# Banded attention with a new schedule: values transposed, q and k halves swapped by DMA, clearing in parts

## The reference

```python
q = _apply_rope(proj(Wq, bq))      # 16 heads of 64 features
k = _apply_rope(proj(Wk, bk))      # rot = concat([-x2, x1]); x*cos + rot*sin
v = proj(Wv, bv)
# block of 128 queries against the block before and its own (256 keys), band mask
scores = einsum('bhnqd,bhnkd->bhnqk', qb, kcat) * scale
attn = softmax(where(valid, scores, -1e30))
ctx = einsum('bhnqk,bhnkd->bhnqd', attn, vcat)
return merged @ Wo.T + bo
```

## Time and profile before

| | us |
|---|---|
| median of 3 runs | 1757.1 (1752.41 to 1758.5) |
| the profiled execution | 1754.96 |
| its span, first to last instruction | 1753.2 |
| window stage, within the span | about 57 to 890 |

### The profile page before, as it was taken

How to read it: one execution, slowest core, us unless ns; L and a number is a source line. 1 busy time by engine, 2 the same in 40 slices (tenths; PEclk the granted TensorE clock), 3 DMA queues, 4 the chain that set the end, 5 groups by cost and what they waited for, 6 DMA issues and landing times. The chain is left out here.

```text
span 1753.2 us, 34607 instructions
## 1 busy us (share of the span) xinstructions
PE 1382.8 (79%) x9686; PEld 1165.0 (66%) x9686; DVE 1069.7 (61%) x3844; ACT 860.1 (49%) x1810; POOL 729.3 (42%) x725
## 2 busy tenths in 40 slices
PE   0799999999999999999944189962997974269791
PEld 0478787887878788787843188861584863258791
DVE  5566666666666666666667355538685877434553
ACT  1355555555555565656544044431684764134450
POOL 4355454545454555454537534540000005724451
PEclk9899999999999999999965599985998985579896
DMA  4899980000000000000031112213000001112125
GB/s 161 145 207 201 203 171 0 0 0 0 0 0 0 0 0 0 0 0 0 0 107 53 49 54 63 60 31 95 1 1 1 0 1 40 52 52 61 53 60 145
DMA packets 129148, 90.63 MB, mean 52 GB/s; under 512 B 9196, under 2 KB 121983, under 8 KB 128818
## 3 DMA queue, kind: packets, MB, share of 16 engines
q1 hardware_dynamic: 118560, 70.73, 18.9%
q0 software_dynamic: 9216, 16.94, 2.9%
q10 hardware_dynamic: 1298, 2.13, 0.4%
HBM read 30.28 MB, written 61.57 MB: 52 GB/s over the span
## 5 line engine op out<-in xcount | busy, mean ns | idle before, releaser
L598 ACT ACTIVATE sc<-sc,mx 128x256 f32<-128x256 f32 x516 | 234.4, 501 | 329.6 <-DVE mx L666 329.6
L765 POOL TENSOR_TENSOR rot<-rot,sin 128x512 f32<-128x512 f32 x132 | 209.5, 1587 | 365.3 <-DVE rot L675 365.3
L666 DVE CUSTOM_DVE_ANT_0 sc<-ps,mask 128x256 f32<-128x256 f32 x516 | 197.7, 420 | 185.8 <-PE ps L506 183.2
L529 PEld LDWEIGHTS po<-V,pT 128*128 128x128 f32 x2048 | 255.4, 193 | 5.3
L529 PE MATMUL po<-V,pT 128*128 128x65 f32 x2048 | 258.6, 269 | 0.0
L887 POOL DMA_INDIRECT yt<-yo,xt x160 | 160.2, 1001 | 205.3 <-DVE yo L987 175.8
L423 POOL DMA_INDIRECT xg<-xw,slot x128 | 124.9, 976 | 289.6 <-DVE slot L285 254.3
L506 PE MATMUL ps<-K,Q 64*128 64x256 f32 x1032 | 196.6, 431 | 0.8 <-DVE mx L666 0.7
L516 PE MATMUL pt<-ident,sc 128*128 128x128 f32 x1028 | 169.5, 288 | 13.9 <-ACT sc L598 13.9
L516 PEld LDWEIGHTS pt<-ident,sc 128*128 128x128 f32 x1028 | 108.1, 141 | 103.7 <-issue 59.3
L947 ACT ACTIVATE hT<-ph,b 128x256 f32<-128x256 f32 x320 | 125.8, 477 | 87.9 <-PE ph L910 87.9
(11 more groups left out here) (181 smaller groups left out, 2708.5 us busy)
## 6 DMA issues: line engine op xcount, KB each, us to landing
xg<-zeros SPq DMA_DIRECT2D x76, 520.0 KB, 9.7
xt<-xg SPq DMA_DIRECT2D x80, 130.0 KB, 2.1
got<-yt SPq DMA_DIRECT2D x32, 256.0 KB, 5.2
yt<-yo,xt POOLq DMA_INDIRECT x160, 2.3
x<-in_hidden SPq DMA_DIRECT2D x8, 256.0 KB, 8.4
w<-in_w SPq DMA_DIRECT2D x1, 2048.0 KB, 9.4
xg<-xw,slot POOLq DMA_INDIRECT x128, 2.3
out_x<-x SPq DMA_DIRECT2D x8, 256.0 KB, 4.3
```

Of the source, the lines that this page charges most:

```text
L529: ins = nc.tensor.matmul(po[:, b // 2, (b % 2 * 2 + h) * VCOLS:(b % 2 * 2 + h + 1) * VCOLS], pT[:, b % 2, h, kb, :], V[:, c, b + kb, h, :] ...
L598: nc.scalar.activation(sc[:, b % 2, h, :], sc[:, b % 2, h, :], ACT.Exp, scale=-1.0, bias=mx[:, b % 2, h:h + 1]).then_inc(S["p"], 1)
L666: nc.vector.tensor_tensor_reduce(sc[:, b % 2, h, :], ps[:, h, 0:2 * P], (mask0 if b == 0 else mask)[:, :], -float(HD) ** -0.5, 3e38, ALU.a ...
L765: nc.gpsimd.tensor_tensor(rot[:, which, :], rot[:, which, :], s.sin[:, pos(sb)], ALU.mult).then_inc(S["pool"], 1)
```

## The change

**Values and normalising.** V becomes the stationary operand (64 columns of a head) and the transposed probabilities the moving one (128 columns); the outputs of the two heads lie on partitions 0 to 63 and 64 to 127 of `po`, already transposed. V loses its column of ones; the sums come from the exponentials' accumulator (`ls`). DVE inverts them (`invert`, 128x8), POOL copies each over 64 columns (`spread`, 128x512 into `rb`), PE transposes that (`turn_sums`, block 3, into `pj`), ACT copies it to `rT` (`read_sums`), and DVE multiplies `po` by it once a unit (`normalise`, block 0 of the next unit), into `oT`. `project_out` moves to block 3 of the next unit. The bias of v is added in `keep_v`, that of the output by POOL (`add_bias`, 128x512, once in 8 units), and `start_out` goes.

**Order.** `scores` and `maxima` run three blocks ahead, with four buffers of `sc` instead of two; `project_q`, `project_k`, `project_v` stand in blocks 0, 1, 2.

**Rotation.** The host's permutation goes. The halves of 32 partitions are swapped by four DMAs of 32 partitions x 2 KB on SP's queue, for q and for k of each unit (`swap_halves`), from `lin` to `rot`. `lin` times cos goes to a tile of its own, `lc`. POOL's `rotate` is as before; `spread` stands between that of q and that of k.

**Clearing.** One DMA in each unit (`clear`, 5 or 4 blocks of 130 KB), behind the unit's swaps on SP's queue; 64 in all, the same bytes. SP also loads v's bias (512 KB) and the output's (64 KB), broadcast over the partitions, ahead of the stage.

```diff
             def project_q(v, c, sb, head=False):
-                pe.wait_ge(S["v_sb"], START + v + CHUNKS)
-                if not head:
-                    pe.wait_ge(S["oT_sb"], START + v - 1)
+                if head:
+                    pe.wait_ge(S["v_sb"], START + v + CHUNKS)
+                else:
+                    pe.wait_ge(S["r_sb"], START + v - 2)
...
+                    pe.wait_ge(S["norm"], START + u)
+                for kb in range(2):
+                    for h in range(2):
+                        ins = nc.tensor.matmul(po[h * HD:(h + 1) * HD, c % 2, b * P:(b + 1) * P], V[:, c, b + kb, h, :],
+                                               pT[:, b % 2, h, kb, :], start=(kb == 0), stop=(kb == 1))
                 ins.then_inc(S["pv"], 1)
...
+            def turn_sums(u):
+                pe.wait_ge(S["rb"], START + u + 1)
                 pe.wait_ge(S["v_sb"], START + u + 3 + CHUNKS)
...
+                    ins = nc.tensor.transpose(pj[:, t * P:(t + 1) * P],
+                                              rb[:, t, :, :].rearrange("p h d -> p (h d)"), s.ident[:, :])
+                ins.then_inc(S["r"], 1)
...
-                pe.wait_ge(S["oT_sb"], START + u + 2)
+                pe.wait_ge(S["norm"], START + u + 2)
...
+                        if b == 0:
+                            scores(c, 3, u, G + 3)
                         else:
-                            scores((c + 1) % CHUNKS, b - 2, u + 1, G + 2)
+                            scores((c + 1) % CHUNKS, b - 1, u + 1, G + 3)
                         transposes((b + 1) % SB_TILES, G + 1)
                         if b == 0:
-                            turn_out(u - 1)
+                            if vc == 0:
+                                pe.wait_ge(S["xl"], START + vsb + 1)
+                            project_q(v, vc, vsb)
+                        if b == 1:
+                            project_k(v, vc, vsb)
                         if b == 2:
-                            project_out(u - 1, (c - 1) % CHUNKS, sb)
-                            project_k(v, vc, vsb)
-                        if b == 3:
-                            project_v(v, vc)
-                        values(c, b, u, G)
-                        if b == 1:
                             if vc == 0:
                                 pe.wait_ge(S["xs"], START + vsb + 1)
-                                pe.wait_ge(S["xl"], START + vsb + 1)
-                            project_q(v, vc, vsb)
-            turn_out(CHUNKS * NSB - 1)
+                            project_v(v, vc)
+                        if b == 3:
+                            turn_sums(u)
+                            project_out(u - 1, (c - 1) % CHUNKS, sb)
+                        values(c, b, u, G)
...
+                    nc.scalar.activation(sc[:, b, h, :], sc[:, b, h, :], ACT.Exp, scale=-1.0,
+                                         bias=mx[:, b, h:h + 1],
+                                         accum_out=ls[:, c % 2, b, h:h + 1]).then_inc(S["p"], 1)
...
+            def read_sums(u):
+                act.wait_ge(S["r"], START + u + 1 + CHUNKS)
+                act.wait_ge(S["norm"], START + u + 1)
+                nc.scalar.copy(rT[:, :], pj[:, :]).then_inc(S["r_sb"], 1)
...
                         if b == 0:
-                            read_out(u - 1, (c - 1) % CHUNKS)
+                            read_q(v, vc)
                         if b == 1:
-                            read_q(v, vc)
-                        if b == 3 and c == 2:
+                            read_k(v, vc)
+                        if b == 2 and c == 2:
                             act.wait_ge(S["k_ps"], START + CHUNKS * sb)
                             high_x(sb + 1)
-                        if b == 2:
-                            read_k(v, vc)
-            read_out(CHUNKS * NSB - 1, CHUNKS - 1)
+                        if b == 3:
+                            read_sums(u)
...
+                    dve.wait_ge(S["t"], START + G - 3)
...
-                nc.vector.tensor_tensor(lin[:, which, :], lin[:, which, :], s.cos[:, pos(sb)], ALU.mult).then_inc(
+                nc.vector.tensor_tensor(lc[:, which, :], lin[:, which, :], s.cos[:, pos(sb)], ALU.mult).then_inc(
                     S["q_cos" if which == 0 else "k_cos"], 1)
...
+                nc.vector.tensor_tensor(V[:, c, 1:, :, :].rearrange("p t h d -> p t (h d)"),
+                                        pj[:, :].rearrange("p (t d) -> p t d", t=SB_TILES),
+                                        s.bv[:, c, :].unsqueeze(1).to_broadcast([P, SB_TILES, P]),
+                                        ALU.add).then_inc(S["v_sb"], 1)
+            def invert(u, c):
+                dve.wait_ge(S["p"], START + 2 * SB_TILES * (u + 1))
+                nc.vector.reciprocal(rs[:, c % 2, :, :], ls[:, c % 2, :, :]).then_inc(S["rs"], 1)
+            def normalise(u, c):
+                dve.wait_ge(S["pv"], START + SB_TILES * (u + 1))
+                dve.wait_ge(S["out"], START + u + 1)
+                dve.wait_ge(S["r_sb"], START + u + 1)
+                nc.vector.tensor_tensor(oT[:, :], po[:, c % 2, :], rT[:, :], ALU.mult).then_inc(S["norm"], 1)
...
-                        maxima(c, (b + 2) % SB_TILES, G + 2)
                         if b == 2:
-                            turn(v, vsb, 0, "q_sb", False)
-                            turn(v, vsb, 1, "k_sb", False)
-                        if b == 3:
+                            invert(u, c)
+                        maxima(c, (b + 3) % SB_TILES, G + 3)
+                        if b == 0:
+                            normalise(u - 1, (c - 1) % CHUNKS)
+                            if c == 1:
+                                add_out(sb)
+                        if b == 1:
+                            times_cos(v, vsb, 0)
+                        if b == 2:
+                            times_cos(v, vsb, 1)
                             keep_v(v, vc)
...
+            def swap_halves(v, which, w0=False):
+                sp.wait_ge(S["k_sb" if which else "q_sb"], START + v + 1)
+                stand_alone(sp, s)
+                if not w0:
+                    sp.wait_ge(S["k_rdy" if which else "q_rdy"], START + v + (CHUNKS if which else 0))
+                stand_alone(sp, s)
+                for h in range(4):
+                    to, of = h * HD // 2, (h ^ 1) * HD // 2
+                    sp.dma_start(rot[to:to + HD // 2, which, :], lin[of:of + HD // 2, which, :]).then_inc(
+                        S["k_sh" if which else "q_sh"], 16)
...
+            def clear(sb, c):
+                n, r = ZERO_PART * (c % 4), min(ZERO_PART, ZERO_TURN - ZERO_PART * (c % 4))
+                part = s.xg[c // 4].rearrange("j (r p) d -> p (j r) d", p=P)
+                sp.dma_start(part[:, bass.ds((sb * ZERO_TURN + n) * (GROUP // P), r * GROUP // P), :],
+                             s.zeros[:, :].unsqueeze(1).to_broadcast([P, r * GROUP // P, ROW])).then_inc(s.s_zeroed, 16)
...
+            for v in range(2):
+                swap_halves(v, 0, v == 0)
+                swap_halves(v, 1, v == 0)
+            with sp.Fori(0, NSB) as sb:
+                for c in range(CHUNKS):
+                    u, v, vc, vsb = units(sb, c)
+                    swap_halves(v, 0)
+                    swap_halves(v, 1)
+                    clear(sb, c)
...
-                pool.wait_ge(S["q_sh" if which == 0 else "k_sh"], START + v + 1)
+                pool.wait_ge(S["q_sh" if which == 0 else "k_sh"], START + 64 * v + 64)
...
-                nc.gpsimd.tensor_tensor(K[:, c, P:] if which else Q[:, c % QBUF, :], lin[:, which, :],
+                nc.gpsimd.tensor_tensor(K[:, c, P:] if which else Q[:, c % QBUF, :], lc[:, which, :],
                                         rot[:, which, :], ALU.add).then_inc(S["k_rdy" if which else "q_rdy"], 1)
-            def unit(v, c, sb):
-                pool.wait_ge(S["oT"], START + v + 1)
+            def spread(u, c):
+                pool.wait_ge(S["rs"], START + u + 1)
+                pool.wait_ge(S["r"], START + CHUNKS + u)
+                stand_alone(pool, s)
+                nc.gpsimd.tensor_copy(rb[:, :, :, :], rs[:, c % 2, :, :].unsqueeze(3).to_broadcast(
+                    [P, SB_TILES, 2, HD])).then_inc(S["rb"], 1)
...
                 rotate(v, c, sb, 0)
+                if spreads:
+                    spread(v - 2, (c - 2) % CHUNKS)
                 rotate(v, c, sb, 1)
```

More of the change, by code:

```diff
@@ L37 @@
 PART = 8
-ZERO_DMAS = XBLOCKS // 4
+ZERO_TURN = XBLOCKS // NSB
+ZERO_PART = -(-ZERO_TURN // 4)
+ZERO_DMAS = NSB * CHUNKS
 ROW = HID + 2
@@ L459, in window_stage @@
         S = s.signals["window"]
-        swap = [(w + 16) % 32 for w in range(32)]
         block = ctx.enter_context(nc.Block())
@@ L525, in values @@
                 if b == 0:
-                    pe.wait_ge(S["norm"], START + 2 * u)
-                for h in range(2):
-                    for kb in range(2):
```

(52 more changed lines are left out.)

112 lines of the change are left out of this document (47 added, 65 removed).

## The result

The changed kernel takes 1797.8 us (median of 4 runs, 1793.8 to 1801.4) against 1757.8 before on the same chip: a ratio of 1.023, 95% interval 1.020 to 1.026, **slower by 40 us**. The range held it, the forecast of 1761 was 37 us short.

What follows compares the result with a forecast made beforehand. TensorE's own order of work was taken to bound the kernel, 12.54 us a unit. 64 x (12.60 - 12.54) = +4, +1.5, -1.4 on 1754.96 gave 1759, median 1761 us; eight in ten: 1720 to 1812.

Steps and rivals of the forecast that it cites:

- The loop that decides: From project_q through ACT, SP, DMA, POOL and turn_sums to the next project_q: 8.49 + 4.11 = 12.60 us a unit.
- The issues: Three DMA issues on SP ahead of q's last one, 0.45 us each: 1.35 us, bounds 1.0 and 1.45.
- The landing: From the last DMA issue of q's swap to its data in place: 1.65 us, bounds 1.5 and 2.1.
- SP's wake: SP wakes after ACT's copy of q, passes a second wait and two increments: 0.40 us, bounds 0.2 and 0.6.
- ACT's read: ACT's read of q, counted from the end of project_q: 0.95 us.
- Granted clock still 1.00: Expected in the changed kernel's profile: TensorE's granted clock stays at its full 2.4 GHz level.
- Rival 3: PE's values run one head after the other, 1.1 us: unit 12.95, 1783 us, chance 0.12; with open loads 1876, chance 0.03.
- k's chain: k's swap and rotation, POOL done at about 11.2 us, due 13 us in: hidden by 2 us.
- Head and tail: Outside the loop: +1.5 us for the two units ahead of it, -1.4 us at the last output.
- rival 1: Shorter chain (issues 0.37, landing 1.5, POOL undisturbed): unit 12.1 us, 1729 us, from 1707 to 1751, chance 0.25.
- rival 2: Longer chain (landing 2.1, issues 0.48, both POOL products disturbed): unit 13.3 us, 1806 us, chance 0.15.
- Rival 4: PE stays the bound at 11.4 us a unit, the chain no loop: 1684 us, chance 0.02.

Runs made afterwards that it cites:

- spread first: The changed kernel with POOL's spread moved ahead of the rotation of q: 1658.1 us, ratio 0.945 to the kernel before.
- two queues: The changed kernel with two of the four DMAs that swap q issued by ACT, the other two by SP: 1715.9 us, ratio 0.977 to the kernel before.
- project_out first: The changed kernel with project_out ahead of turn_sums in PE's program: 1723.6 us, ratio 0.981 to the kernel before.
- six small products: The changed kernel with six unused matmuls of 128 columns ahead of PE's wait for rb: 1793.1 us, ratio 1.021 to the kernel before.

## Why the prediction was right or wrong

- **The loop that decides**: right. PE waits before turn_sums for `rb` in every unit, and the loop closes through ACT, SP, DMA and POOL. Up to turn_sums it takes 8.77 for 8.49, PE's own work 7.1 for 7.3, so the wait is 1.7 for 1.2. Moving one line of POOL's order opened it; shortening it by two issues or by project_out moved the unit by 1.28 and 0.89.
- **The issues**: mis-sized. 0.45 was set from single issues; in a series on one queue they start 0.63 apart. That is +0.55 a unit, and above my upper bound of 1.45 for the three.
- **The landing**: 2.0 against 1.65. I took less than the earlier trace rows for a smaller transfer within SBUF. The Trainium skill's fixed cost of about 2.0 us (DMA: Bandwidth & Descriptors, Anatomy of one DMA, where it stands for DMAs issued by GpSimd) was the better guide to the landing, and these DMAs of SP agree: 1.9 to 2.2. The 12.95 a unit that followed from it overshot the measured 12.75 because the other terms were 0.75 too high together and the issues 0.55 too low.
- **SP's wake, ACT's read**: 0.39 too long together. **POOL**: DVE's cosine product began before POOL's product, not behind it, so the product and not the sum stretched (1.86 and 1.21 for 1.47 and 1.67); the sum of both was right to 0.1. Spread and its wake, and PE's stretch, 0.06 and 0.13 too long. In all +0.15 a unit: 10 us.
- **What comes once in 8 units**: not counted for the changed kernel. The 12.54 before is a mean that holds start_out; 12.60 was one for ordinary units only. The turns of ACT's loop added 7.5 us to it, the first units of the loop 1.6.
- **"Granted clock still 1.00"**: wrong, and the largest miss, 25 of the 37 us. I had priced PE's wait as time lost and nothing else. With a wait in each unit the granted clock fell now and then, and the slowed work lay on the same loop. With the wait filled, the falls left the ordinary units; with a longer wait they came in all.
- **"ACT's exponentials also write their sums ... room too"**: right for the ordinary unit, wrong at the turn of the loop, where the 64 added instructions make the body long. I put the 7.5 us there down to that; taking the long body away was worth 13 us (1658.1 to 1645.0) once PE was the bound.
- **Values**: 0.59 for 0.75, two heads at once, as the Trainium skill's page TensorEngine Tiling (Array Packing), Key Properties, has it; project_v, the same eight records without it, takes 0.98. Rival 3 fell. Since PE had slack, it brought nothing here; with spread first, 4 x (0.98 - 0.59) = 1.6 us of each unit rest on it.
- **The clears, k's chain, the longer lead of maxima**: cost nothing, as said. A clear lands 5.1 us behind its issue, not 3.3, which is still before the next swaps, and these land in 1.9 to 2.2 throughout. **Head and tail**: -4.5 where I had +0.1. The loop part of the kernel before was 1.2 above 63 x 12.54. With this the misses are 9.5 + 24.8 + 7.5 + 1.6 - 4.6 - 1.2 = 37.6 us, as measured on the profiled executions.
- **Sums**: the low ends add up to 7.55 and 11.4, not 7.4 and 11.3; rival 1's terms to 12.0, not 12.1; rival 2's, with a product stretched by 0.24, to 13.4 or more, not 13.3. Nothing above hangs on them.
- **The rivals**: rival 2 (a longer chain, 1806) came nearest in time, at a unit of 12.75, not 13.3; the rest of its time was the clock and the turns. So it was partly luck that the range of 1720 to 1812 held the time: its upper end stood for a longer chain and for values one head at a time, and two thirds of the miss came from the clock, which no rival had. Rival 4's end, PE as bound, needed no shorter chain but a loop cut open; I saw "spread queued behind rotate" and did not ask what moving it would give.

What stays open: what exactly makes the clock fall in one unit and not in the next. In the changed kernel ten of the 16 falls lie in units that are otherwise ordinary, with the same wait of 1.68 us as in the units without one; six lie at a turn or among the first units. In the kernels with two queues (0.3 us of waiting a unit), with project_out first (0.85) and with six small products (0.4) no ordinary unit has a fall. Theirs, four, two and five, lie at a turn of a loop, but for one among the first units, and all but one of them have an idle of PE of 1.4 to 2.3 us just ahead. With 3.9 us of waiting a unit every unit has one.

## What to carry to other kernels

When an operation is moved to DMA, look for what stands behind its wait on the engine that consumes it: here one small copy queued behind the wait closed a loop around TensorE, and its place in the order was worth 140 us while the swap's own price was nothing. Price a swap by DMAs as count x issue pitch + one landing, and fewer, larger ones win. A wait that returns on TensorE can cost more than its length when the clock reacts to it, as 1.7 us in each unit did here and 0.85 did not, so a chain that comes out "about even" should be forecast as slower.

## What the runs showed of the hardware

- A series of small DMAs within SBUF from SP: 0.58 us an issue, 0.63 from start to start, whether 64 or 32 KB; landing 2.0 and 1.9 us.
- The clock falls to 1.2 GHz for 3.4 us at a time though PE's longest idle in the unit, at 442 us for one, was 1.7 us; a fall on the critical loop cost 1.55 us.
- At the turn of a loop ACT stands still for 2.5 to 3.1 us with a body of 316 recorded instructions (2.4 to 4.3 in the other kernels with it), for 0.2 with one of 252 or 167. PE (weight loads and control, matmuls not counted) stands 2.0 to 2.4 us with a body of 1004, mostly with a fall of the clock, and not at all with one of 908 or 915; with 940 it was up to 3.8. The instruction queues on the page (ACT 87 against 46 packets, PE 90 against 27) tell it at a glance.
- Reading the exponentials' accumulator is an instruction of its own, 0.19 us.
- Two heads' matmuls on the two halves of the columns overlap in either order: eight records in 0.59 us.
